# First batch, key-side turns and unread products rearranged in a four-layer macaron kernel

## The reference, cut to what matters

```
ffn0:  logits = norm(x) @ router_w.T; softmax; top 2 of 8; tokens are gathered
       to their experts, run through two products and added back
attn1: 16 heads of 8 numbers; q, k, v = x @ W + b; q, k rotated (rope);
       softmax(q k^T / sqrt(8)) @ v; @ Wo + bo
attn2: 16 heads of 64 numbers; softmax(q k^T * 64**-0.5 + alibi, causal) @ v; @ Wo + bo
attn3: 16 heads of 8 numbers; softmax(q k^T * scale) @ v, without rotation or Wo
```

## Time and profile before

| | us |
|---|---|
| median of three timed executions | 2635.18 |
| lowest and highest of them | 2627.62, 2643.91 |
| the profiled execution, its own time | 2625.39 |
| its span, first to last instruction | 2623.7 |
| outside the span | 1.7 |
| TensorE, VectorE, ScalarE, GpSimd busy, share of the span | 83%, 74%, 68%, 38% |

### The profile page before, as it was taken

The page is one execution under the profiler, slowest core; times in us unless marked ns, Lnnn a source line. Parts: engine busy times, 40 slices in busy tenths (PEclk is TensorE's granted clock), DMA queues, the critical chain, the costliest instruction groups (busy, mean ns, idle before and its releaser), DMA issues. The chain is left out here.

```text
span 2623.7 us, 47720 instructions
## 1 busy us (share of the span) xinstructions
PE 2190.3 (83%) x15155; PEld 1122.4 (43%) x15155; DVE 1943.4 (74%) x5751; ACT 1793.1 (68%) x4548; POOL 998.2 (38%) x1519
## 2 busy tenths in 40 slices
PE   3868786658888879599999999997868888888888
PEld 2446454412222236344444444445334444444453
DVE  4547637769899958677777778767678888888766
ACT  2234324338788774478887878885489999999965
POOL 2644363354464432600000000006655555555537
PEclk8789596769999997799999999999889999999999
DMA  4420514024224200100000000000020011111001
GB/s 141 115 83 22 149 47 129 8 44 87 53 55 87 55 11 1 33 1 2 2 1 2 1 2 2 2 1 1 7 65 18 17 34 33 33 33 33 1 1 33
DMA packets 227640, 94.85 MB, mean 36 GB/s; under 512 B 175746, under 2 KB 215490, under 8 KB 227394
## 3 DMA queue, kind: packets, MB, share of 16 engines
q1 hardware_dynamic: 220864, 83.46, 13.0%
q0 software_dynamic: 3584, 7.58, 1.0%
q10 hardware_dynamic: 2946, 0.77, 0.1%
HBM read 30.66 MB, written 19.17 MB: 19 GB/s over the span
## 5 line engine op out<-in xcount | busy, mean ns | idle before, releaser
L2348 DVE TENSOR_REDUCE s_neg_max<-s_ps_a 128x1 f32<-128x512 f32 x1024 | 661.2, 683 | 142.7 <-PE s_ps_a L2151 130.3
L2623 ACT ACTIVATE s_pT<-s_ps_t 128x512 f32<-128x512 f32 x1024 | 644.3, 660 | 119.2 <-PE s_ps_t L2185 99.2
L2614 ACT ACTIVATE s_first<-s_ps_a,s_neg_max 128x512 f32<-128x512 f32 x512 | 411.9, 805 | 13.9 <-DVE s_neg_max L2348 13.6
L2539 POOL TENSOR_SCALAR s_first<-s_first,s_rec 128x512 f32<-128x512 f32 x384 | 300.9, 799 | 283.3 <-DVE s_rec L2354 283.1
L2197 PE MATMUL s_ps_t<-ident,s_first 128*128 128x128 f32 x2048 | 313.7, 284 | 64.0 <-ACT s_pT L2623 51.1
L2993 DVE CUSTOM_DVE_ANT_0 s_e<-s_ps_a,w_alibi 128x128 f32<-128x128 f32 (+3 forms) x512 | 225.7, 488 | 127.2 <-PE s_ps_a L2829 126.8
L2151 PE MATMUL s_ps_a<-s_lanesT 64*128 64x512 bf16 x1024 | 270.4, 398 | 37.0 <-DMA s_lanesT<-n_lanes 21.4
L2197 PEld LDWEIGHTS s_ps_t<-ident,s_first 128*128 128x128 f32 x2048 | 220.6, 141 | 160.7 <-ACT s_pT L2623 117.2
L2215 PE MATMUL s_ps_o<-s_pT,n_v_pad 128*32 128x512 f32 x2048 | 272.8, 606 | 12.3 <-ACT s_oT L2629 12.3
L3101 ACT ACTIVATE s_e<-s_e,s_neg_max 128x128 f32<-128x128 f32 (+3 forms) x512 | 281.9, 563 | 0.0
L3109 ACT ACTIVATE s_pT<-s_ps_t 128x384 f32<-128x384 f32 (+1 forms) x320 | 156.3, 532 | 115.4 <-PE s_ps_t L2856 89.4
(11 more groups left out here) (430 smaller groups left out, 4134.2 us busy)
## 6 DMA issues: line engine op xcount, KB each, us to landing
s_y_rows<-s_zeros SPq DMA_DIRECT2D x4, 2048.0 KB, 10.4
s_parts<-s_y_rows SPq DMA_DIRECT2D x32, 256.0 KB, 4.0
s_token_rows<-s_rows SPq DMA_DIRECT2D x2, 2176.0 KB, 10.5
s_Wi<-L_ffn_experts_inter SPq DMA_DIRECT2D x2, 1792.0 KB, 15.6
x<-L_attn_x SPq DMA_DIRECT2D x4, 512.0 KB, 8.3
out<-x SPq DMA_DIRECT2D x8, 256.0 KB, 2.3
s_lanesT<-n_lanes SPq DMA_TRANSPOSE x64, 4.6
s_shiftedT<-n_lanes SPq DMA_TRANSPOSE x64, 2.4
```

The lines of the kernel that those rows point to most:

```text
L2348: dve.tensor_reduce(neg_max[:, column(n):column(n) + 1], sa[n % NA][:], AX.X, ALU.max, negate=True).then_inc(s.max_ready, 1)
L2539: do.free(pool.tensor_scalar(f, f, rec1[:, n:n + 1], 1.0, ALU.mult, ALU.mult))
L2614: act.activation(first[:, g % NF, n % PU, :], sa[n % NA][:], ACT.Exp, bias=neg_max[:, n:n + 1], accum_out=sum1[:, n % (NR * PU):n % (NR * ...
L2623: act.activation(pT[:, n % NP, :], st[n % NK][:], ACT.Exp).then_inc(s.probs_ready, 1)
```

## The change

Setup: after its last transposition TensorE issues ten unread products. Routing: five unread products instead of two behind each of the first two batches' transpositions.

Narrow attention: weights, biases and the rest count on three semaphores. ScalarE scales the weight as soon as the three weights are there, and the bias after its copy of the input; TensorE, VectorE and GpSimd wait for their part. In attn1 the first batch is rotated by VectorE; the low parts of that batch are made by VectorE, the copies of high by GpSimd, the copies of middle by ScalarE.

Wide attention: the scores of tile 3 stand before `by_keys(g, 1)`. `by_keys(g, 1)` writes `st` instead of `st[1]` and `vo_ps`; `by_keys(g, 2)` writes the score banks `sa[0]`; q and k are projected into `sa[1]`. ScalarE's first exponentials stand before its copies of `by_keys(g, 1)`. The waits follow the banks.

```diff
--- before.py
+++ after.py
@@ setup, tensor
                 turn_adapters(pe)
+                pe.wait_ge(s.made, 2)
+                stir(pe, G, psC[:], 10)
@@ capacity_experts_ffn, tensor
-                    stir(pe, G, slots_ps[0][:], 2)
+                    stir(pe, G, slots_ps[0][:], 2 if b > 1 else 5)
@@ narrow_prepare
+    loaded, rest = 16 * 3, 16 * (len(loads) - 6)
     def load(sp):
-        for to, of in loads:
+        for to, of in loads[:3]:
             sp.dma_start(to, of).then_inc(s.nw_loaded, 16)
+        for to, of in loads[3:6]:
+            sp.dma_start(to, of).then_inc(s.nb_loaded, 16)
+        for to, of in loads[6:]:
+            sp.dma_start(to, of).then_inc(s.rest_loaded, 16)
-    def scale_queries(act):
-        act.wait_ge(s.nw_loaded, loaded)
-        for w in (G.nw, G.nb):
-            act.activation(w[:, 0:D], w[:, 0:D], ACT.Copy, scale=scale).then_inc(s.nw_scaled, 1)
+    def scale_queries(act, w, here):
+        act.wait_ge(here, loaded)
+        act.activation(w[:, 0:D], w[:, 0:D], ACT.Copy, scale=scale).then_inc(s.nw_scaled, 1)
@@ narrow_attention: sync, tensor
+                    if once and j == 0:
+                        sp.wait_ge(s.mid_copied, 2)
...
                 def output(j):
+                    if j == 0:
+                        pe.wait_ge(made.rest_loaded, rest)
@@ narrow_attention: vector
                     if j == 0 and t == 0:
-                        dve.wait_ge(made.nw_loaded, loaded)
+                        dve.wait_ge(made.nb_loaded, loaded)
...
+                def rotate_first():
...
+                    dve.wait_ge(made.rest_loaded, rest)
+                    dve.wait_ge(s.qkv_added, TB)
+                    do.free(dve.tensor_tensor(ra[:], x1, cos, ALU.mult))
+                    do.free(dve.tensor_tensor(rb[:], x2, sin, ALU.mult))
+                    do(dve.tensor_tensor(rc[:], x1, sin, ALU.mult))
+                    do(dve.tensor_tensor(x2, x2, cos, ALU.mult))
+                    do.free(dve.tensor_tensor(x2, rc[:], x2, ALU.add))
+                    do(dve.tensor_tensor(x1, ra[:], rb[:], ALU.subtract))
+                    dve.engine_nop().then_inc(s.rotated, 1)
...
-                    elif step == 3 and not once:
+                    elif step == 3 and (not once or j == 0):
                         do.free(dve.tensor_tensor(q_slot(j, of("l", 0)[0]), qkv[:, 0], q_slot(j, MID), ALU.subtract))
-                    elif step == 4 and not once:
+                    elif step == 4 and (not once or j == 0):
                         do.free(dve.tensor_tensor(k_slot(j, of("l", 1)[0]), qkv[:, 1], k_slot(j, MID), ALU.subtract))
...
+                if once:
+                    rotate_first()
                 for step in range(once, 6):
                     split(0, step)
@@ narrow_attention: gpsimd
-                    if once and which:
+                    if once and which and j:
...
-                    pool.wait_ge(made.nw_loaded, loaded)
+                    pool.wait_ge(made.rest_loaded, rest)
...
-                    rotate(0, 0)
-                    rotate(0, 1)
+                    pool.wait_ge(s.rotated, 1)
@@ narrow_attention: scalar
-                scale_queries(act)
+                scale_queries(act, G.nw, made.nw_loaded)
                 copy_xnT(0, sa[0][:])
+                scale_queries(act, G.nb, made.nb_loaded)
...
                     split_high(0)
+                    act.wait_ge(s.mid_ready, 1)
+                    for side, i in ((q_slot, of("m", 0)[0]), (k_slot, of("m", 1)[0])):
+                        act.activation(side(0, i), side(0, MID), ACT.Copy).then_inc(s.mid_copied, 1)
@@ wide_attention: banks
-        q_ps, k_ps = sa[0]
+        q_ps, k_ps = sa[1]
...
-        HALF_ORDER = (1, 0)
-        turn_bank = lambda m, half: vo_ps if (m, half) == (1, 0) else st[half]
+        turn_bank = lambda m, half: sa[0][half] if m == len(TURNS) - 1 else st[half]
@@ wide_attention: tensor, project_q
-                        pe.wait_ge(s.max_ready, PU * (g - 1) + 6)
+                        pe.wait_ge(s.max_ready, PU * g)
@@ wide_attention: tensor, by_keys
                     if m == 1:
-                        j, r = divmod(g, PB)
-                        if g:
-                            pe.wait_ge(s.pair_ready, g)
-                        else:
-                            pe.wait_ge(s.xnT_ready, 2)
-                        if r == 1 and j:
-                            pe.wait_ge(s.x_added, j)
-                        if r == 5 and j + 2 < B:
-                            pe.wait_ge(s.xnT_ready, j + 3)
-                    n = TU * g + (0, 1, 3)[m]
-                    if n:
-                        pe.wait_ge(s.probs_ready, n)
+                        pe.wait_ge(s.probs_ready, TU * g + 2)
+                    if m == 2 and g + LAG < PAIRS:
+                        pe.wait_ge(s.max_ready, PU * (g + LAG) + 6)
+                    elif m == 2:
+                        pe.wait_ge(s.max_ready, UNITS)
@@ wide_attention: tensor, products and v_product
+                        if g:
+                            pe.wait_ge(s.pair_ready, g)
                         pe.wait_ge(s.v_copied, min(g + 1, 2 * TB * (B - 1)))
-                    pe.wait_ge(s.probs_ready, TU * g + 2 * min(max(kt, 1), len(TURNS) - 1) + 2)
+                        if j and pair >= 1:
+                            pe.wait_ge(s.x_added, j)
+                    pe.wait_ge(s.probs_ready, TU * g + 2 * min(kt, len(TURNS) - 1) + 2)
...
-                    pe.wait_ge(s.probs_ready, TU * n + 4)
+                    if n:
+                        pe.wait_ge(s.pair_ready, n)
@@ wide_attention: tensor, the loop over pairs
                         scores(g + LAG, 2)
+                        scores(g + LAG, 3)
                     by_keys(g, 1)
-                    if ahead:
-                        scores(g + LAG, 3)
                     by_keys(g, 2)
@@ wide_attention: scalar, the loop over pairs
-                    copy_probs(g, 1)
                     if ahead:
                         exps(g + LAG, 0)
+                    copy_probs(g, 1)
                     copy_probs(g, 2)
```

22 lines of the change are left out of this document (14 added, 8 removed).

## The result

The changed kernel took 2596.72 us in the median of seven executions (2595.87 to 2611.79), the kernel before 2627.86 in the same rounds and those shown ahead (2620.05 to 2643.91, seven executions). The ratio is 0.9887, with a 95% interval of 0.9862 to 0.9913. The profiled execution took 2596.50, 28.9 less than the profiled one of before; its span is 2594.8.

The account below looks back on a forecast made before the run. It took TensorE, busy 83% of the span, to set wide attention's pace, and a one-engine-at-a-time chain the first narrow attention's start. Terms -9.5 - 8.9 - 0.7 - 7.5 + 0.7 = -25.9 gave 2599.5, plus 3.5: 2603 us, range 2588 to 2620.

Parts of the forecast that it names:

- the carry: Whole kernel: 3.5 us added to the sum because the profiled execution was faster than the timed ones.
- Wide attention: Wide attention: reordered pairs less the costs in the last batch and at the start, -9.5 us, between -15 and +4.
- the steady pairs: Wide attention, g = 1 to 55: the new order gains 0.25 us a pair, 13.7 us.
- The last batch: Wide attention's last batch: project_q must wait for tile 3's reading, +0.55 in five pairs, 2.7 us.
- At the start: Wide attention's start: the first project_q steps wait for tile 3's reading, +1.5 us, between 0 and 3.
- Rival 2: Wide attention: the new wait on VectorE eats the pair's gain, stage at +4, total 2617; chance 0.18.
- rival 3: Wide attention: TensorE's writes into neighbouring score banks hold up VectorE's reading of tile 3, total 2672; chance 0.04.
- (a): First narrow attention: weights issued first, so ScalarE's 3.05 us wait goes; 2.8 us earlier.
- (b): First narrow attention: VectorE rotates instead of GpSimd, 4.3 us instead of 7.7; 3.4 us earlier.
- (c): First narrow attention: split from ScalarE's high part to the transposition takes 5.9 us instead of 8.6; 2.7 earlier.
- GpSimd's four copies are hidden: First narrow attention's split: GpSimd's copies of high end 3.85 us after their start, hidden below VectorE's work.
- Rival 1: Second routing: the clock stays at 0.50, +3.2 us instead of -7.5, total 2614; chance 0.12.

Follow-up runs that it names:

- e2: Kernel before with the changes to the two narrow attentions alone; 2638.68 us, ratio 0.9961.
- e8: Changed kernel with an idle 0.48 us VectorE memset ahead of its reading of tile 3 in each wide-attention pair; 2643.74 us.
- e12: Changed kernel with GpSimd again rotating the first batch of the first narrow attention; 2602.86 us in one execution.
- e11: Changed kernel with each ffn0 routing's five unread products behind the last two batches' transpositions instead of the first two's; 2617.81 us in one execution.
- e1: Kernel before with the change to wide attention alone; 2648.70 us, ratio 0.9994.
- e6: Changed kernel with the first value product ahead of project_q in wide attention's last batch; 2624.05 us.
- e5: Changed kernel unaltered, run again; 2629.36 us against 2646.79 of the kernel before, ratio 0.9920.
- e9: Changed kernel with last-batch value product ahead of project_q, and five unread products behind the last stage's first two batches; 2598.50 us, ratio 0.9870.

## Why the prediction was right, step by step

The forecast was 2603, the range 2588 to 2620, the time is 2596.7. The sum without the carry was 2599.5, and the profiled execution took 2596.5.

**Wide attention**, forecast -9.5, measured -7.4, of which the varying start of the stage is part. Term by term: the steady pairs gave 11.0 and not 13.7. The steps within the pair came where they were laid: `by_keys(g, 1)` 2.82 (forecast 2.8), `by_keys(g, 2)` 3.22 (3.26), the value product 3.74 to 3.77 (3.75), `project_q` 4.65 (4.66). What I left out is that behind it not everything keeps its distance. From the value product to the next scores there were 5.90 us (1401.90 to 1407.80) and are now 5.94. In the medians of the ordinary pairs it is 5.89 and 5.94, and the value product stands 0.23 earlier instead of 0.25, so an ordinary pair gains 0.18 and the average pair 0.20: this is the missing 2.7. Why, the trace does not say. The step from `project_q` to the next products grew from 0.96 to 1.01 and the one from the output to the next scores from 0.96 to 0.99, the one behind the products shrank by 0.03, and none shows a wait. The last batch cost 2.9 (forecast 2.7): its five countable periods are 48.40 instead of 45.47. At the start, the distance between the first scores of the first two pairs is 10.06 or 10.07 in all ten profiles with the new order (8.84 or 8.85 in the four without it), and that between the second and the third 7.5 (7.1): +1.6, forecast +1.5. Not foreseen are two gains: the first period of the loop is 13.3 instead of 14.9 in the medians of these profiles, and the stage's end, where no scores are ahead, 0.9 shorter. The very start, up to the first scores, takes 10.7 to 13.6 us with the new order and 12.1 to 13.6 with the old; in the two profiles compared it was 1.4 longer after. It is 13.6 in eight of the ten profiles with the new order, and in e2 with the old one, so whether the change has a part in it is not shown. Together -11.0 + 2.9 + 1.6 - 1.5 - 0.9 + 1.4, the -7.4 of the table (1.5 is the first period's share in these two).

**Rival 2** (the new wait on VectorE eats the gain) is refuted by the 0.20 that each steady pair gained, although its mechanism is real: VectorE releases `by_keys(g, 2)` in every pair, and e8 leaves `project_q` a room of 0.11, the margin of 0.1 that was forecast. In the rival's sum 13.7 stands for the difference of +4 and -9.5, which is 13.5 and gives 2616.5. Refuted too is **rival 3** (VectorE held up by TensorE's writes into neighbouring banks), by the rows of tile 3: its halves are 0.69 long with `by_keys(g, 2)` beside them, as before. The Trainium skill's sentence cited there speaks of ScalarE and VectorE beside each other, at full bandwidth where no bank is shared, and not of TensorE's writes; it did not by itself make the rival's case empty. These rows do.

**First narrow attention**, forecast -8.9, measured -9.6. (a) The bias additions end 11.55 after the stage's start instead of 14.69, -3.1 (forecast -2.8). (b) From there to ScalarE's high part 4.1 us instead of 7.8, -3.7 (-3.4): VectorE's six operations are 0.69 each, the value that I took, not the 0.97. e12 shows it by itself. (c) From the high part to the transposition 6.1 instead of 8.6, -2.5 (-2.7). These make -9.3; the rest of the -9.6 lies behind the first scores. In the medians over all profiles (e12 left out) the stage is 438.8 instead of 448.0, 9.2 less.

The Trainium skill spoke for -7.6 here ("SBUF — State Buffer", "SBUF: two separate sides": the one that starts first holds the port for the whole instruction). The two low parts ran back to back in 0.97 and 0.98 beside GpSimd's copies, and the chain gained what it had to without that price. But the remainder ahead of them does what the rule says. Where GpSimd starts 0.04 ahead of VectorE (and e12 again), the remainder takes 1.65; where VectorE starts 0.03 ahead of GpSimd, in the changed kernel, it takes 1.23 and the four copies 4.71 instead of 3.85. The first of these copies takes 1.67 when it starts second and 0.61 when it starts first. e12's rows:

```profile
533.27 1.65 DVE L2358 TENSOR_TENSOR s_qkv<-s_qkv,n_lanes 128x1024 f32<-128x1024 f32 x1 [8.98 <-ACT n_lanes L2678]
```

```profile
533.23 4.19 POOL L2524 COPY n_lanes<-n_lanes 128x512 bf16<-128x512 bf16 x4 [1.22 <-ACT n_lanes L2678]
```

So my step "GpSimd's four copies are hidden" narrowly failed: with 4.71 they end at 531.41, behind VectorE's last low part (530.94), and SyncE issues at 531.62, behind them. In e12 VectorE is last. The time from the high part's start to the transposition is 6.1 in the one and 6.0 in the other: the order in which the two engines start decides who pays, hardly how much.

**Second narrow attention**: -1.0, forecast -0.7 with an end at -0.8. The bias additions end 0.9 earlier, where I had counted only the wait that the row names.

**The routings**: second -8.2, forecast -7.5 (19.2 against 20.0). The mechanism is as put: the clock is lifted and the rest runs at the first routing's pace. Rival 1 (it stays at 0.50) is refuted by ten profiles, in each of which the second routing is under 19.4; all four kernels without five products in front have over 27. My argument against that rival rested on a misreading, though: I took the 1.00 of the earlier trace rows to mean that the first routing had the clock up from its start. It began at the lower level and came back with two products a batch, which seven of fifteen such stretches did. First routing -0.3 (forecast +0.5), setup +0.15 (+0.2). The products in the first routing are not hidden: the three profiles of its cases give 16.67 for a low start with two products, 15.82 for a high one with two and 16.38 for a high one with five (before, e11, after). So the setup's ten bring 0.85 and the six more take back 0.56.

**The step that was wrong is the carry.** I took the profiled execution to be lucky by 10 us against its median, and put 3.5 of that on the changed kernel as well. The profiles show what the scatter is: the kernel before loses 10.7 us more when its first routing runs at the lower level too (e1), and some 12 when the last stage stays there (e1: 96.93 against 84.55; 15 in e6 against e5). The 1.7 us by which the last stage differs in the two profiles compared are of the same kind: it began low and came back in the one, and began at the upper level in the other. The change takes away the first of these, as far as ten profiles with five products show, and leaves the second. Its seven times are five near 2597 and two near 2611, with a mean granted clock of 0.932 to 0.935 in the five and 0.926 and 0.927 in the two. That fits a last stage at the lower level in those two; neither was profiled, so it is not shown. The medians happened to differ by 31, about as much as 2603 stands below the 2635 given; with e5's chip the difference was 17. Part of the closeness is luck: the parts that the change touches came to -26.4 in the two profiles, against -25.9 forecast, because wide attention fell short by 2.1 and the narrow attentions, setup and routings together gave 2.5 more; the stages that it doesn't touch gave another 2.5; and the carry of 3.5 did not show. How often each stretch falls cannot be told from fourteen profiles.

**A better version.** e6 is worth 3.7 us of wide attention in each of three profiles. e9 adds to it the steady last stage.

## What to carry to other kernels

Read the stages apart, and compare each with the same stage in several profiles, before a difference of the whole is explained: here unchanged stages moved by 10 to 15 us between executions, about as much as the largest part of the change. When two waits change places, lay the new order on the old times and measure the room of the new wait with a pause of known length (e8: 0.48 in, 0.37 at the step that waits, 0.21 in the period). Read the effect at the step itself as well as in the period, since what lies behind it may give some of the time back, and put the pause ahead of each wait that is to be measured. A gap between a releasing row and the released one is not all room (0.26, of which 0.15 stood there also when the step waited). And look for the iterations that lack the filler, such as the last batch, where the room is gone. Filler work for the clock is worth what it brings forward, so it belongs at the very front of a stretch that would else run at the lower level.

## What the runs showed of the hardware

**A full TensorE does not lift its clock by being full.** In a routing with two unread products a batch TensorE is busy for 27.37 of 27.41 us and stays at 1.2 GHz throughout (e1, e2), and so does e6's last stage (27.36 of 27.40). Two products a batch can be enough, as they were in seven of fifteen stretches: the last stage of the kernel before was at the lower level too, with 1.03 for its first four transpositions, and came back within the first of the router-like products, to 0.95 for eight of them:

```profile
2538.51 1.06 PE L178 MATMUL s_ps_y<-ident 128*128 128x512 bf16 x2
2539.36 1.01 PE L691 MATMUL s_ps_l<-gateT,s_xT 128*128 128x8 f32 x8
```

e6's had the same order of the same products at nearly the same pace up to that point (1.09 for the first four), and did not come back; so with two it is left to something that these profiles do not show, and a stretch that has missed this point stayed low to its end in every profile. Three more unread products behind each of two batches brought it to 2.4 GHz in all fourteen stretches that had them in front, at the earliest within the first group and at the latest right behind the second, and in the back as well (e11). The Trainium skill ("TensorE: Matmul & The Clock Gate", "Part 1: The HAM clock gate") has the clock set by how busy TensorE has been of late; by that rule, taken as the profile's busy time, these stretches would have come back to 2.4 GHz, and the rows say they did not. The busy time that the profile counts did not decide it here.

**The clock column can be wrong at the beginning of a program.** In e1's first routing the window says 1.00, but the products run at the slow pace. The eight products of the router's take 1.72, as the 1.71 of the second routing at 0.50 and not the 0.95 of a routing at 1.00:

```profile
38.33 1.72 PE L874 MATMUL s_ps_up<-routerT,s_xnT 128*128 128x8 f32 x8
```

The first routing of the kernel before is such a case too: a window from 34.20 to 38.40 says 1.00, over transpositions that take 1.09 and 1.06. So the level is to be read from durations of the same form wherever the span has just begun.

**Other starts vary as well.** Beside the three stretches of the table, the first narrow attention varies at its start. With the new code its bias additions end 11.2 to 11.6 us after the start in four profiles and 12.6 to 12.7 in six. Wide attention's start varies by up to 2.9 with the same code. What sets them at the moment a stage begins was not tried.
